# An attention product in rounded halves, one item later, and a query weight loaded in two parts, in a graph transformer kernel

## The reference

```python
routing_input = x.mean(axis=1)
logits = jax.nn.relu(routing_input @ r_w1 + r_b1) @ r_w2 + r_b2
sel = jnp.argmax(jax.nn.softmax(logits, axis=-1), axis=-1)
...
scores = jnp.einsum('bhqd,bhkd->bhqk', q, k) / jnp.sqrt(jnp.float32(D_K))
attn = jax.nn.softmax(scores, axis=-1)
out = jnp.einsum('bhqk,bhkd->bhqd', attn, v)
out = out.transpose(0, 2, 1, 3).reshape(B, S, D_MODEL)
return out @ wo
```

```python
out = jnp.einsum('btn,btd,nde->bte', attn, x, value_weight)
```

## Time and profile before

| | |
|---|---|
| median of 3 runs | 2493.89 us |
| lowest and highest | 2493.52 and 2495.85 us |
| the profiled execution's own time | 2496.94 us |
| its span, first to last instruction | 2495.1 us |
| TensorE busy | 2382.2 us, 95% of the span |
| DVE busy | 1749.0 us, 70% |
| POOL busy | 1602.4 us, 64% |
| ACT busy | 919.5 us, 37% |
| mean granted clock of TensorE | 0.981 of full |

### The profile page before, as it was taken

One profiled execution on the slowest core, in us unless ns is written; L12 is line 12 of the kernel. 1 busy time (PEld: TensorE's weight loads), 2 busy tenths in 40 slices (PEclk: granted clock), 3 DMA queues, 4 the chain that ended last, 5 costly groups with the idle time before them and its releaser, 6 DMA issues.

```text
span 2495.1 us, 33879 instructions
## 1 busy us (share of the span) xinstructions
PE 2382.2 (95%) x11420; PEld 1972.0 (79%) x11420; DVE 1749.0 (70%) x2511; ACT 919.5 (37%) x1097; POOL 1602.4 (64%) x720
## 2 busy tenths in 40 slices
PE   6989979888999699999999999999999999999999
PEld 5878868776999577777777777777777777777777
DVE  8984235347998787777777777777777777777775
ACT  2841226622998622232323232232322322223221
POOL 0023413348887577777777777777777777777773
PEclk9998979999999999999999999999999999999999
DMA  3014110023444111212121212121212121212111
GB/s 77 20 55 158 46 68 18 1 77 76 122 103 110 40 68 68 101 67 101 67 101 67 101 67 101 67 101 67 101 67 101 67 100 68 97 71 94 74 68 38
DMA packets 49885, 190.85 MB, mean 76 GB/s; under 512 B 13300, under 2 KB 17911, under 8 KB 33444
## 3 DMA queue, kind: packets, MB, share of 16 engines
q1 hardware_dynamic: 35728, 177.90, 20.5%
q0 software_dynamic: 13200, 10.75, 2.1%
q10 hardware_dynamic: 900, 1.44, 0.2%
HBM read 177.54 MB, written 12.35 MB: 76 GB/s over the span
## 4 chain that ended last, share of the span: by engine, by line
PE 80%; DVE 13%; ACT 4%; issue 1%; POOL 1%; DMA 1%; SPq 0%; DVEq 0%; ACTq 0%; POOLq 0%
PE PS L1650 25%; PE PS L1651 24%; PE PS L1652 24%; PE PS L1861 2%; PE PS L1728 2%; DVE msgl L1456 2%; ACT msgh L1022 1%; DVE hotS L1149 1%; DVE hotD L1150 1%; DVE PS L1480 1%; DVE PS L1484 1%; DVE PS L1485 1%; DVE PS L1487 1%; DVE negmax L1363 1%; ACT PT L986 1%
## 5 line engine op out<-in xcount | busy, mean ns | idle before, releaser
L1594 DVE SCALAR_TENSOR_TENSOR XN<-PS,attn,XN 125x512 f32<-125x512 f32 x1083 | 804.6, 748 | 440.6 <-PE PS L1652 440.5
L789 POOL TENSOR_TENSOR OPl<-TS,OPh 128x1024 fp32r<-128x1024 f32 x256 | 679.0, 2653 | 123.6 <-ACT OPh L1041 116.8
L789 POOL TENSOR_TENSOR OPl<-RAW,OPh 128x1024 fp32r<-128x1024 f32 x192 | 556.8, 2900 | 256.6 <-ACT OPh L1041 256.6
L1650 PE MATMUL PS<-OPh,XVh 128*125 128x512 f32 x1280 | 508.0, 397 | 0.0
L1652 PE MATMUL PS<-OPh,XVl 128*125 128x512 f32 x1280 | 502.0, 392 | 0.0
L1651 PE MATMUL PS<-OPl,XVh 128*125 128x512 f32 x1280 | 501.1, 391 | 0.0
L1041 ACT ACTIVATE OPh<-TS 128x1024 fp32r<-128x1024 f32 x256 | 272.2, 1063 | 533.2 <-PE PS L1652 519.2
L1041 ACT ACTIVATE OPh<-RAW 128x1024 fp32r<-128x1024 f32 x192 | 203.6, 1061 | 583.3 <-PE PS L1652 577.2
L1650 PE MATMUL PS<-OPh,Sh 128*125 128x512 f32 x1024 | 404.0, 395 | 10.3 <-DVE XN L1591 10.1
L1652 PE MATMUL PS<-OPh,Sl 128*125 128x512 f32 x1024 | 404.7, 395 | 0.0
L1651 PE MATMUL PS<-OPl,Sh 128*125 128x512 f32 x1024 | 404.2, 395 | 0.0
(11 more groups left out here) (301 smaller groups left out, 3196.8 us busy)
## 6 DMA issues: line engine op xcount, KB each, us to landing
RAW<-in_values SPq DMA_DIRECT2D x64, 2048.0 KB, 7.7
filters<-filt SPq DMA_DIRECT2D x14, 672.0 KB
fil<-filters SPq DMA_DIRECT2D x11, 840.0 KB
Wraw<-in_ffn SPq DMA_DIRECT2D x4, 1024.0 KB, 6.0
Wraw<-in_L_q SPq DMA_DIRECT2D x2, 1024.0 KB, 5.0
Wraw<-in_L_k SPq DMA_DIRECT2D x2, 1024.0 KB, 8.3
Wraw<-in_L_v SPq DMA_DIRECT2D x2, 1024.0 KB, 7.2
gatW<-nodes,dstI POOLq DMA_INDIRECT x90, 3.4
```

What stands on the lines that cost most here:

```text
L789: g.tensor_tensor(OPl[:, j], operand_source(j, parity), OPh[:, j].bitcast(F32), ALU.subtract).then_inc(op_lower, 1)
L1594: v.scalar_tensor_tensor(out=XN[:, t], in0=PS[0:P, bank, :], scalar=w, in1=XN[:, t], op0=ALU.mult, op1=ALU.add).then_inc(v_added, 1)
L1650: mm(dst, lh, rh, start=start, stop=False, skip_group_check=resumed)
```

## The change

The attention product no longer multiplies plain float32. The values go to VS, which holds for each pair of heads the columns [high of the even head, low of the even head, low of the odd head, high of the odd head], 64 each; ACT writes the high ones and DVE the low ones. The transposed probabilities go to PTh (ACT) and PTl (DVE). A product is now 10 matmuls in float32r, PTh and PTl in turn against 128 columns of VS, and its result has the high values' part in 64 partitions and the low values' part in the other 64. ACT rounds the first part into XTh; DVE subtracts that from the first part and then adds the second part, in two instructions, the second of which waits for the first. `probT` and `v1` leave BY_SCALAR, so their slots are now free when DVE is done with them. Each product comes one item later, and there is one more step.

F_q is loaded as two halves of 256 columns, and ACT and DVE (no longer POOL) split it in four slices of 128 columns; `q1` waits for one slice at a time.

XVh and XVl are gone: the anchor loop reads its tiles of 125 from XTh and XTl, which have no gaps between tiles, and Sh and Sl lose their gaps too.

```diff
-ATTENTION_STEPS = ITEMS + LAG + 1
+ATTENTION_STEPS = ITEMS + LAG + 2
...
-    if turned > 0 and turned % T == T - 2:
+    if turned > 0 and turned % T == T - 1:
         parts.append(("attn", turned // T * 2))
-    if turned > 0 and turned % T == 0:
+    if turned >= T and turned % T == 1:
         parts.append(("attn", turned // T * 2 - 1))
...
-BY_SCALAR = {"score", "v1", "probT", "qT2", "ov1"}
+BY_SCALAR = {"score", "qT2", "ov1"}
...
-                sp.dma_start(Wraw[SIDE[w]][:], src).then_inc(w_loaded[SIDE[w]], 16)
+                if name == "F_q":
+                    sp.dma_start(Wraw[SIDE[w]][:, :, 0:D // 2], src[:, :, 0:D // 2]).then_inc(query_half, 16)
+                    sp.dma_start(Wraw[SIDE[w]][:, :, D // 2:D], src[:, :, D // 2:D]).then_inc(w_loaded[SIDE[w]], 16)
+                else:
+                    sp.dma_start(Wraw[SIDE[w]][:], src).then_inc(w_loaded[SIDE[w]], 16)
...
-            weight_upper(WEIGHT["F_q"])
+            w = WEIGHT["F_q"]
+            wait_filled(WEIGHTS[SHARER[w]][1])
+            act.wait_ge(query_half, 16)
+            for f in range(K):
+                c = slice(f * 128, (f + 1) * 128)
+                if f == K // 2:
+                    act.wait_ge(w_loaded[SIDE[w]], 16 * LOADS[w])
+                a.activation(Wh[SIDE[w]][:, :, c], Wraw[SIDE[w]][:, :, c], ACT.Copy).then_inc(query_upper, 1)
...
+            for f in range(K):
+                c = slice(f * 128, (f + 1) * 128)
+                dve.wait_ge(query_upper, f + 1)
+                v.tensor_tensor(Wl[SIDE[w]][:, :, c], Wraw[SIDE[w]][:, :, c], Wh[SIDE[w]][:, :, c].bitcast(F32),
+                                ALU.subtract).then_inc(query_lower, 1)
...
-                    a.activation(PT[:, :, c], turned_tiles(u), ACT.Copy).then_inc(drained_s, 1)
+                    upper(u, PTh[:, :, c], turned_tiles(u))
...
-                        rest(u, halves(XTl[o:o + 64, head // 2])[:, h], slot(u)[o:o + 64, 0, 0:HN], halves(XTh[o:o + 64, head // 2])[:, h])
+                        turned_l, low = halves(XTl[o:o + 64, head // 2])[:, h], 64 - o
+                        dve.wait_ge(upper_ready, splits(u))
+                        link(v.tensor_tensor(turned_l, slot(u)[o:o + 64, 0, 0:HN],
+                                             halves(XTh[o:o + 64, head // 2])[:, h].bitcast(F32), ALU.subtract))
+                        v.tensor_tensor(turned_l, slot(u)[low:low + 64, 0, 0:HN], turned_l.bitcast(F32), ALU.add).then_inc(drained_v, 1)
...
+                    if part == "probT":
+                        c = tile_columns(n % T)
+                        rest(u, PTl[:, :, c], turned_tiles(u), PTh[:, :, c])
...
-                        ins = mm(slot(u)[:, 0, 0:HN], VF[:, t, c], PT[:, t, queries], start=t == 0, stop=t == T - 1)
+                        mm(slot(u)[:, 0, 0:HN], VS[:, t, head // 2, c], PTh[:, t, queries], start=t == 0, stop=False)
+                        ins = mm(slot(u)[:, 0, 0:HN], VS[:, t, head // 2, c], PTl[:, t, queries], start=False, stop=t == T - 1)
...
                 def plain(t, k):
-                    return XVh[:, k, t, 0:P], XVl[:, k, t, 0:P]
+                    c = tile_columns(t)
+                    return XTh[:, k, c], XTl[:, k, c]
```

More of the change, by code:

```diff
@@ L51 @@
 ANCHORS = 128
-BELOW_SH = 8
 DUOS = ANCHORS // 2
@@ L142, with by_whole @@
 SLOT_USER = {u: max((e for e in range(n) if SLOT[UNITS[e]] == SLOT[u]), default=None) for n, u in enumerate(UNITS)}
+def by_whole(w):
+    return w + 1 - (w >= WEIGHT["F_q"])
 def unit_ending(stage, t):
@@ L369, in build @@
             attnsum = sb("attnsum", [P, T], F32, late)
-            sb("below_OPh", [128, 16], F32, late)
+            sb("below_OPh", [128, 24], F32, late)
             OPh = sb("OPh", [128, OPERANDS, 2, D], F32R, late)
@@ L487, in turned_tiles, with value_parts, by_parity @@
             return slot(unit)[0:P].rearrange("p b (t n) -> p (b t) n", n=128)[:, 0:T, 0:P]
+        def value_parts(t):
+            pieces = VS[:, t].rearrange("p q (g d) -> p q g d", d=DH)
+            return pieces[:, :, 0:4:3], pieces[:, :, 1:3]
+        def by_parity(rows):
+            return rows.rearrange("p (q e d) -> p q e d", e=2, d=DH)
         def keys_low(head):
@@ L634, in _ @@
                     move_rows(sp, nodes.rearrange("(j p) f -> p j f", p=P), hnode[:], nodes_stored)
-                sp.wait_ge(w_split, SHARER[w] + 1)
+                if name_of(SHARER[w]) == "F_q":
+                    sp.wait_ge(query_lower, K)
+                else:
+                    sp.wait_ge(w_split, by_whole(SHARER[w]))
                 if name_of(w) == "F_q":
@@ L746, in _ @@
                         g.tensor_tensor(X[:, j], X[:, j], XN[:, j], ALU.add).then_inc(x_silu, 1)
-                split_weight(w)
+                if name_of(w) != "F_q":
+                    split_weight(w)
             split_weight(WEIGHT["F_o"])
@@ L973, in _ @@
                     wait_filled(u)
-                    a.activation(VF[:, tiles[0]:tiles[-1] + 1], slot(u)[0:P, 0:len(tiles), :], ACT.Copy).then_inc(drained_s, 1)
+                    for i, t in enumerate(tiles):
+                        ins = a.activation(value_parts(t)[0], by_parity(slot(u)[0:P, i]), ACT.Copy)
+                    ins.then_inc(upper_ready, 1)
                 if part == "attn":
@@ L1063, in _ @@
                 a.activation(XF[:, :, tile_columns(j)], turned, ACT.Copy).then_inc(s_copied, 1)
-                upper(u, XVh[:, :, j, 0:P], turned)
+                upper(u, XTh[:, :, tile_columns(j)], turned)
             for j in range(T):
@@ L1070, in _ @@
                 act.wait_ge(s_summed, n + 1)
[L1071 removed]
+                a.activation(Sh[:, j], SF[:, j], ACT.Copy).then_inc(s_upper, 1)
             act.wait_ge(sq_ready, 1)
@@ L1132, in transposed_rest @@
                         v.tensor_copy(XTl[:, :, N:NT], XTl[:, :, N - 1:N].bitcast(F32).to_broadcast([128, K, NT - N])).then_inc(drained_v, 1)
-                    elif stage == "xt3":
-                        rest(u, XVl[:, :, j, 0:P], ins, XVh[:, :, j, 0:P])
                     else:
@@ L1357, in _ @@
                 ins.then_inc(drained_v, 1)
-            v.memset(PT[:, :, N:NT], 0.0).then_inc(pt_padded, 1)
+            v.memset(PTh[:, :, N:NT].bitcast(F32), 0.0)
+            v.memset(PTl[:, :, N:NT].bitcast(F32), 0.0).then_inc(pt_padded, 1)
             for i in range(ATTENTION_STEPS + 1):
@@ L1695, in node_columns @@
                     begin(u)
-                    if f == 0:
-                        pe.wait_ge(w_split, w + 1)
+                    if stage == "q1":
+                        pe.wait_ge(query_lower, f + 1)
+                    elif f == 0:
+                        pe.wait_ge(w_split, by_whole(w))
                     c = slice(f * 128, (f + 1) * 128)
@@ L1854, in _ @@
                     head, h = n // 2, n % 2
-                    u, c, queries = ("attn", n), slice(head // 2 * 128, head // 2 * 128 + 128), slice(h * HN, (h + 1) * HN)
+                    u, c, queries = ("attn", n), slice(head % 2 * 128, head % 2 * 128 + 128), slice(h * HN, (h + 1) * HN)
                     begin(u)
```

43 lines of the change are left out of this document (22 added, 21 removed).

## The result

| | before | after |
|---|---|---|
| median | 2494.87 us (4 runs on the same chip) | 2513.99 us (4 runs) |
| lowest and highest | 2493.52 and 2499.34 | 2510.01 and 2514.28 |
| the profiled execution's own time | 2496.94 us | 2513.85 us |
| its span | 2495.1 us | 2512.0 us |

The ratio is 1.0067, with a 95% interval of 1.0054 to 1.0079: the changed kernel is slower by 0.5 to 0.8%, or 17 us in the middle; the two medians are 19 us apart. The forecast was 9 us slower. Its range ended at 2512 us: the ratio times the forecast's base, 2493.9 x 1.0067 = 2510.6, lies inside it, the median of the four runs 2 us above it.

What follows compares the result with a forecast made beforehand. TensorE, busy 95% of the span, seemed the bound; in attention, who waits for whom. Query weight -6.9, attention +15.8 and loop 0 sum to +8.9 on 2493.9: 2502.8 us, 80% range 2488 to 2512.

Steps and rivals of the forecast that it cites:

- The query weight, -6.9: F_q's load and split before q1: halves and slices let q1 start 6.9 us earlier (5.3 to 8.1).
- The attention, +15.8: Attention stage: TensorE's waits for DVE's PTl make it 15.8 us longer, a head 15.29 us for 13.18.
- 0.46 to the next matmul: Attention: time taken for a set of transposes before the next matmul, in the step behind a product.
- The steps behind a product: Attention, negmax to next negmax after a step with a product: 2.91 us, where it was 1.19 before.
- the fifth step: Last step of a head in the attention: 1.56 us from negmax to negmax, set by DVE alone.
- The filling: Start of the attention: the ten value rests on DVE cost nothing, lying in time when DVE was idle.
- I take 0: Anchor loop: tiles at multiples of 500 bytes, not 512, change nothing; possible -3.5 to +9.7 us.
- the +9.7 end: Anchor loop: upper bound of its term, 6912 matmuls at 0.2333 us each.
- Rival 1: Attention: transposes behind a product need not wait for the previous item's PTl; a head 12.59 us, total 2482; 14%.
- Rival 2: Attention: rests and handovers overlap better, stage only +7 to +10 us, total 2494 to 2497, counted as same; 12%.
- Rival 3: Attention: the clock falls in TensorE's idle stretches, half clock costing +50 us; total 2527 to 2553; 7%.
- Rival 4: Anchor loop: it slows by 9.7 us, total 2512; 5%.

Runs made afterwards that it cites:

- no_rest: The changed kernel with PTl zero and no DVE instruction for it, the slot free once ACT has copied it: 2482.42 us, ratio 0.9941 to the kernel before.
- reordered: The changed kernel, all work kept; TensorE does transposes, scores, then product, and DVE does PTl and the product's rests before negmax: 2477.75 us, ratio 0.9932.
- query_only: The kernel before with the change of F_q alone (two transfers, four slices on ACT and DVE): 2489.78 us, ratio 0.9972.
- plain_packed: The kernel before with the anchor loop's tiles of 125 read from XTh and XTl, without gaps: 2502.41 us, ratio 1.0023.
- both_shifted: The kernel before with the tiles of XVh, XVl, Sh and Sl 12 bytes to the right in their fields: 2469.52 us, ratio 0.9896.
- rests_first: The changed kernel with PTl and the product's rest before the next negmax on DVE, TensorE's order unchanged: 2526.52 us, ratio 1.0113.

## Why the prediction was right, and where its sizes were off

- **The direction and the mechanism: right. The size is low by half.** TensorE waits for product, scores, negmax and PTl in a row; no_rest and reordered take away that chain in two ways and the 18.9 us go, with 12 to 14 more. Span against span the change costs 16.9 us where +8.9 was forecast: 3.1 of the difference lie in the attention, 5.5 in the anchor loop and 2.4 between them, and 3.0 went the other way, before the first scores.
- **The query weight, -6.9: right.** query_only gives -7.0. In the changed kernel issue to scores shrank by 8.05: q1 started 5.14 us after the issue and not 5.5, since the half landed 0.5 us sooner than I took, and q1 ran less long at half clock (0.82 in the mean over 350.5 to 359, 1.00 behind it), the gain that I had named and not counted.
- **The attention, +15.8: under-sized, it is +18.9.** Three pieces were short.
  The transposes: "0.46 to the next matmul" was read from transposes that follow other work, as here in the changed kernel:

```profile
437.07 0.71 PE L1913 MATMUL PS<-ident,prob 125*125 125x125 f32 x5
437.54 0.39 PE L1890 MATMUL PS<-keys_high,queries_both 128*125 128x314 f32 x1
```

  Behind a wait it is 429.25 - 428.68 = 0.57. The first matmul: behind transposes, or behind a wait, the second starts 0.22 to 0.25 after the first and not 0.147 (429.25 to 429.48, 431.88 to 432.13). So scores to negmax take 0.87 behind transposes for 0.77, and the product 433.42 - 431.88 = 1.54 for 1.47. The steps behind a product thus took 3.08 and not 2.91, those with it 4.07 and 3.95 for 3.99 and 3.92. PTl's slot was free 0.84 us after its start, a little sooner than the 0.88 taken. With the fifth step at 1.63 for 1.56 this head has 15.81 for 15.29. By the means of two heads the growth is 15.71 - 13.29 = 2.4 us a head and not 2.1; the 13.18 that the prediction started from is the shorter of two lengths.
  The filling: the prediction has the rests of the values (ten, where the trace has five) in time in which DVE waits anyway. It left out what waits for them. TensorE does, and from the second to the third negmax it takes 4.1 us more than before. The prediction doesn't list its steps at the ends, so how much of this they held isn't known.
- **The anchor loop, "I take 0": wrong.** It is +5.5 us in the loop here, and plain_packed as a whole is 5.8 slower. The nearest row, the load's 185 ns, says nothing about the spacing: it is 185 ns in the changed kernel and in both_shifted alike. The 60 matmuls with XTh at 0.233, which bore the +9.7 end, were the better witness. Why the spacing is another is open.
- **Between attention and loop, +2.4, not forecast.** 2.6 of it lie at the end of the edge stage, where TensorE idles for 2.7 us before the change and for 2.6 after it, and the clock fell only after it. The first matmul behind the idle time, before and after, then the clock after the change (before, it is 1.00 from 805 to 825 us):

```profile
815.90 0.38 PE L1912 MATMUL PS<-hotE,msgh 125*128 125x314 f32 x1 [2.73 <-ACT hotE L1031]
```

```profile
825.25 0.60 PE L1955 MATMUL PS<-hotE,msgh 125*128 125x314 f32 x1 [2.64 <-ACT hotE L1054]
```

```profile
820.00:824.00 4.00, 2.62 (x18) 2.36 (x17) 3.40 (x6) 4.00 (x6) 0.00 (x0) 1.00 0.00 0
824.00:828.00 4.00, 2.75 (x10) 2.78 (x11) 3.54 (x7) 3.49 (x5) 0.00 (x0) 0.57 0.00 0
```

  The 1.8 us gained before the issue of F_q, where no instruction changed, may be of this kind too (a clock of 0.77 for 0.72 between 185 and 215 us). I have no experiment on either.
- **Rival 1 (short turnaround, faster)** is false for this change and true for reordered: it needs a way around the wait, which the queues as the change wrote them don't have and the reordered ones do. **Rival 2** asked for +7 to +10 and got 18.9. **Rival 3:** from 400 us to the end of the attention the clock stayed at 1.00, at 32.5 of 50 us busy and with idle stretches of 1.7 us. It did fall in the filling, to 0.57 over 394 to 398 us behind the wait for the values: twelve matmuls took 398.50 - 394.06 = 4.44 us, which at 0.231 each are 2.8. It fell in rests_first too. **Rival 4** was half true and came on top of the forecast.

## What to carry to other kernels

When a buffer's release moves to another engine, write out that engine's queue and ask what stands in front of the releasing instruction and who must finish first; here 0.79 us of new work for each of 40 items made the stage 30.7 us longer than it is without it, and with both queues turned the stage, that work included, is 14 us shorter than before the change. Price a step that follows a wait with rows that follow a wait. Where a stage is thousands of equal matmuls, moving an operand by a few bytes is a change of its own: read the spacing of starts, not the durations, and try shifts. Here they gave more than the change had in view, though the rule behind them is not known.

## What the hardware showed that I had not expected

- The spacing of 512-column matmuls in float32r varies with the operands' places in memory from 0.2267 to 0.2333 us, with equal loads (185 ns) and equal durations. A shift of 4 bytes cost 8 us in 6912 matmuls, one of 12 bytes gained 7, and one of 12 bytes for both kinds of tiles gained 27 (2496.21 to 2469.52), more than the whole change cost.
- Five transposes take 0.46 us to the next matmul within work and 0.57 behind a wait, at a granted clock of 1.00 in both. The 0.57 comes behind a wait of 1.68 us as behind one of 0.22 (448.79 to 449.36 in the kernel before).
- In rests_first the granted clock over 400 to 450 us was 0.77 with TensorE busy for 34.4 us, and in the changed kernel 1.00 with 32.5 us busy. Its share of busy time in those 50 us doesn't tell which. Nor does the length of one idle stretch: behind 2.28 and 2.64 us the clock fell in the changed kernel, behind 2.73 us it stayed at 1.00 in the kernel before.
